# Moving tiles stored as even columns, then odd ones, and read by turns in both GEMMs of an f32 feed-forward block

## What is computed

```python
def _L0_cond_ref(x, condition, weights):
    W = weights[condition]                      # (32, 64, 64), a 64x64 matrix for each batch entry
    return jnp.einsum('bct,bcd->bdt', x, W)     # x: (32, 64, 1024)

def _L0_ffn_ref(input, inter_w, inter_b, output_w, output_b):
    h = jax.nn.gelu(jnp.einsum('bsd,df->bsf', input, inter_w) + inter_b, approximate=True)
    out = jnp.einsum('bsf,fd->bsd', h, output_w) + output_b
    return out

x = x + _L0_ffn_ref(_L0_cond_ref(x, itok_B_0_15, L0_cond_weights), ...)
```

## Time and profile before

| what | value |
|---|---|
| median of three runs | 1215.04 us |
| the profiled execution's own time | 1215.01 us |
| its span | 1213.2 us |
| TensorE busy | 1208.7 us, 100% |
| VectorE busy | 884.7 us, 73% |
| ScalarE busy | 562.6 us, 46% |
| matmul instructions in the profile | 5468 |

### The profile page before, as it was taken

The page is one execution under the profiler, slowest core; times in us unless marked ns, Lnnn a source line. Parts: engine busy times, 40 slices in busy tenths (PEclk is TensorE's granted clock), DMA queues, the critical chain, the costliest instruction groups (busy, mean ns, idle before and its releaser), DMA issues.

```text
span 1213.2 us, 15228 instructions
## 1 busy us (share of the span) xinstructions
PE 1208.7 (100%) x5468; PEld 1006.4 (83%) x5468; DVE 884.7 (73%) x1130; ACT 562.6 (46%) x963; POOL 273.4 (23%) x188
## 2 busy tenths in 40 slices
PE   9999999999999999999999999999999999999999
PEld 9888888888888888888888888888888888888887
DVE  5988787778657556665548678577788676788886
ACT  5755555555444444444445444444444444444443
POOL 4351233222306333423301121101110101101000
PEclk9999999999999999999999999999999999999999
DMA  9597667866997544665399998756863749956653
GB/s 347 170 302 250 219 238 288 289 241 219 401 394 234 143 124 125 189 184 138 91 342 306 348 271 266 208 194 157 192 178 115 188 126 243 291 186 179 191 154 107
DMA packets 119868, 267.62 MB, mean 221 GB/s; under 512 B 9938, under 2 KB 19442, under 8 KB 118386
## 3 DMA queue, kind: packets, MB, share of 16 engines
q1 hardware_dynamic: 105248, 232.81, 54.6%
q0 software_dynamic: 13824, 33.56, 16.3%
q10 hardware_dynamic: 722, 0.28, 0.1%
HBM read 174.34 MB, written 92.27 MB: 220 GB/s over the span
## 4 chain that ended last, share of the span: by engine, by line
PE 99%; DMA 0%; DVEq 0%; ACTq 0%; DVE 0%; issue 0%
PE ps L708 50%; PE ps L724 46%; PE ps L656 1%; PE ps L671 1%; PE ps L743 0%; DMA itok_sb<-in_itok_B_dram 0%; DVEq L277 0%; ACTq L918 0%; DVE out L1256 0%; DVE wdiag L1197 0%; DVEq L1197 0%
## 5 line engine op out<-in xcount | busy, mean ns | idle before, releaser
L708 PE MATMUL ps<-y,lhs 128*128 128x512 f32 x2688 | 610.9, 389 | 0.0
L708 PEld LDWEIGHTS ps<-y,lhs 128*128 128x128 f32 x2688 | 504.1, 188 | 104.4
L724 PE MATMUL ps<-rhs,lhs 128*128 128x512 f32 x2472 | 560.5, 389 | 0.0
L724 PEld LDWEIGHTS ps<-rhs,lhs 128*128 128x128 f32 x2472 | 464.0, 188 | 96.4
L901 ACT ACTIVATE lhs<-h_raw 128x512 fp32r<-128x512 f32 x208 | 131.6, 633 | 322.7 <-PE ps L724 317.5
L1091 DVE TENSOR_TENSOR lhs<-h_raw,lhs 128x512 fp32r<-128x512 f32 x208 | 144.2, 693 | 124.8 <-ACT lhs L901 124.6
L994 DVE TENSOR_TENSOR lhs<-w_raw,lhs 128x512 fp32r<-128x512 f32 x128 | 111.2, 869 | 127.7 <-ACT lhs L807 127.7
L807 ACT ACTIVATE lhs<-w_raw 128x512 fp32r<-128x512 f32 x128 | 81.0, 633 | 174.5 <-PE ps L708 172.9
L1094 DVE TENSOR_TENSOR rhs<-w_buf,rhs 128x512 fp32r<-128x512 f32 x208 | 142.4, 685 | 0.0
L906 ACT ACTIVATE rhs<-w_buf 128x512 fp32r<-128x512 f32 x208 | 128.0, 615 | 0.0
L994 DVE TENSOR_TENSOR lhs<-s_w,lhs 128x512 fp32r<-128x512 f32 x96 | 73.0, 765 | 57.4 <-ACT lhs L807 57.0
(11 more groups left out here) (54 smaller groups left out, 553.5 us busy)
## 6 DMA issues: line engine op xcount, KB each, us to landing
h_raw<-p_mem SPq DMA_DIRECT2D x80, 512.0 KB, 5.1
w_raw<-in_L_ffn_inter_w_dram SPq DMA_DIRECT2D x31, 1024.0 KB, 7.9
p_mem<-part SPq DMA_DIRECT2D x96, 256.0 KB, 6.3
w_buf<-in_L_ffn_output_w_dram SPq DMA_DIRECT2D x12, 2048.0 KB, 14.3
q_mem<-part SPq DMA_DIRECT2D x64, 256.0 KB, 6.3
h_raw<-q_mem POOLq DMA_DIRECT2D x32, 512.0 KB, 7.5
y_mem<-y_out SPq DMA_DIRECT2D x28, 512.0 KB, 3.3
y<-y_mem SPq DMA_DIRECT2D x7, 2048.0 KB, 13.5
```

The source lines that it names most:

```text
L708: last = nc.tensor.matmul(ps[:, bank, :], w[:, k, :], y[i][:, part, k, :], start=(i in FRESH and k == 0 and u == 0), stop=(k == KH - 1 and ...
L724: last = nc.tensor.matmul(ps[:, bank2(t, tb), :], lhs[s % RING][:, a, blk(tb)], rhs[r][:, w, :], start=(t in FRESH2 and q == 0 and u == 0) ...
```

## The change

Within each row of 512 words of a moving tile, columns 0, 2, 4, ... now lie first, and columns 1, 3, 5, ... behind them, 256 words (1 KB) further on. `runs` is a stored row seen as its two halves, `by_runs` a row in column order seen as even columns and then odd ones, and `by_pairs` a stored row read back in column order: a word of the first half, a word of the second, and so on. The matmuls of both GEMMs read their moving operand through `by_pairs`, so columns reach TensorE and PSUM in the same order as before. The copies that fill these tiles read their source through `by_runs`, at a step of two words, and write without gaps. For the first half of y the copies out of PSUM do this, so `y_sum`, `y_high` and `y_low` are unchanged; for the second half and for `rhs` the copies and subtractions that split the tile do it. `y1_sum` has three more waits in each of four blocks, on VectorE's own earlier subtractions. The order of the instructions is the same on every engine.

```diff
+        def by_runs(columns):
+            return columns.rearrange("p (b a) -> p a b", a=2)
+        def runs(kept):
+            return kept.rearrange("p (a b) -> p a b", a=2)
+        def by_pairs(kept):
+            return kept.rearrange("p (a b) -> p b a", a=2)
...
-                        last = nc.tensor.matmul(ps[:, bank, :], w[:, k, :], y[i][:, part, k, :],
+                        last = nc.tensor.matmul(ps[:, bank, :], w[:, k, :], by_pairs(y[i][:, part, k, :]),
...
-                        last = nc.tensor.matmul(ps[:, bank2(t, tb), :], lhs[s % RING][:, a, blk(tb)], rhs[r][:, w, :],
+                        last = nc.tensor.matmul(ps[:, bank2(t, tb), :], lhs[s % RING][:, a, blk(tb)], by_pairs(rhs[r][:, w, :]),
...
-                                                        rhs[(r + i) % RING][:, w, cols],
+                                                        by_pairs(rhs[(r + i) % RING][:, w, :])[:, cols.start // 2:cols.stop // 2, :],
...
-                    nc.scalar.activation(to[:, kb % KH, :], ps[:, kb, :], ACT.Copy).then_inc(kept_act, 1)
+                    nc.scalar.activation(runs(to[:, kb % KH, :]), by_runs(ps[:, kb, :]), ACT.Copy).then_inc(kept_act, 1)
...
-                nc.scalar.activation(rhs[r][:, 0, :], w2_part(t, q), ACT.Copy).then_inc(rhs_hi, 1)
+                nc.scalar.activation(runs(rhs[r][:, 0, :]), by_runs(w2_part(t, q)), ACT.Copy).then_inc(rhs_hi, 1)
...
-                nc.scalar.activation(y1_out[item % 2][:, 0, :], y1_in[:, (0, 0, 0, 3, 1, 2, 2)[i], :], ACT.Copy).then_inc(y1_hi, 1)
+                nc.scalar.activation(runs(y1_out[item % 2][:, 0, :]), by_runs(y1_in[:, (0, 0, 0, 3, 1, 2, 2)[i], :]), ACT.Copy).then_inc(y1_hi, 1)
...
-                    nc.vector.tensor_copy(to[:, kb % KH, :], ps[:, kb, :]).then_inc(kept_dve, 1)
+                    nc.vector.tensor_copy(runs(to[:, kb % KH, :]), by_runs(ps[:, kb, :])).then_inc(kept_dve, 1)
...
-                nc.vector.tensor_tensor(rhs[r][:, 1, :], w2_part(t, q), rhs[r][:, 0, :].bitcast(F32),
+                nc.vector.tensor_tensor(runs(rhs[r][:, 1, :]), by_runs(w2_part(t, q)), runs(rhs[r][:, 0, :]).bitcast(F32),
                                         ALU.subtract).then_inc(rhs_lo, 1)
...
+                if n in (0, 1, 3):
+                    dve.wait_ge(y1_split, kb * PRODUCTS + (1, 2, 0, 6)[n])
                 nc.vector.tensor_tensor(y1_in[:, to, :], y1_in[:, a, :], y1_in[:, b, :], ALU.subtract).then_inc(y1_t, 1)
...
-                nc.vector.tensor_tensor(o[:, 1, :], y1_in[:, (0, 0, 0, 3, 1, 2, 2)[i], :], o[:, 0, :].bitcast(F32),
+                nc.vector.tensor_tensor(runs(o[:, 1, :]), by_runs(y1_in[:, (0, 0, 0, 3, 1, 2, 2)[i], :]), runs(o[:, 0, :]).bitcast(F32),
                                         ALU.subtract).then_inc(y1_split, 1)
```

## The result

The changed kernel takes 1165.11 us (median of 4 runs, 1164.06 to 1165.9) against 1214.97 us before: a ratio of 0.9589 (95% interval 0.9572 to 0.9605), or 49.9 us less. The forecast was 2321 us.

The account below looks back on a forecast made before the run. The prediction took TensorE's matmul cadence as the bound: 1215.0 us plus 1105.9 us for the alternating moving read, with zero for copies, waits and writes, gave 2321 us. The range was 1213 to 2425 us, at 80%.

Parts of the forecast that it names:

- The bound: Whole kernel: TensorE busy 1208.7 of 1213.2 us, so time is the number of matmuls times their cadence, plus short ends.
- The split of 226.67 ns: A 512-column matmul in order: 0.4167 ns a word, 213.33 ns, plus 13.3 ns paid once per matmul at either width.
- the price of the moving read: Both GEMMs' matmuls reading alternate halves: 0.833 ns a word instead of 0.4167, adding 1105.9 us; lower bound nothing.
- F: Rival, 7%: faster; the other word order avoids a weight-load collision costing 13.3 ns per matmul, 69 us less, 1146 us.
- B: Rival, 24%: the moving read's stride is free, if the port keeps a line of each half or fetches fast enough; 1215 us.
- D: Rival, 10%: the moving port is late only now and then, giving something between, 1230 to 2146 us.
- E: Rival, 13%: moving read worse than half pace, each line change exposing the whole access; for example 2867 or 4530 us.
- The strided copies: Copies filling moving tiles at a step of two words: zero taken; upper bound 533 ns more on VectorE, 454 on ScalarE.
- part 2: The forecast's step on copies filling moving tiles: zero on the path, with groups staying at 615 and 685 ns.
- C: Rival, 2%: matmul reads free but strided copies slow, about 5 us in GEMM2 and 2 us at the head; 1222 us.
- The copies out of PSUM at the head: At the start, 16 strided copies with thin cover: zero taken; at the upper bound TensorE would wait some 1.9 us.
- The waits on VectorE's own subtractions: Three more per block of y, 12 in all: zero taken; whole subtractions exposed would be 8 us over 200 us.

## Why the prediction was wrong

**The bound.** That TensorE's cadence is the time held nearly: 5178 matmuls times the change of cadence, 55.5 us, is the busy time lost. With the faster cadence 4.8 us of new waits came up beside it.

**The split of 226.67 ns.** 0.4167 ns a word and 13.3 ns a matmul was right: alone, 384, 320 and 256 columns in order take the same 13.1 to 13.4 ns above their words (448 columns take 16.1 ns). It was drawn from one piece of 30 matmuls, so that it held was partly luck.

**The step that failed is the price of the moving read.** I bounded it below by nothing and took 0.833 ns a word from the f32 passes on line 671, on the reason that a contiguous stream can take several neighbouring words with one access and the alternating one "takes that away on every word". By the count of the table, halves by turns lose nothing of that: each of the two lines in use serves four pairs in succession, where in order a line serves two. The price was -10.7 ns a matmul, and my lower bound was on the wrong side of it. The half pace itself is real. It is 431 to 461 ns in the patterns in which a line serves one pair, against my 440 ns; I gave the right price to the wrong pattern.

**The rule of the Trainium skill.** SBUF - State Buffer, in the Trainium skill (the note on cachelines), asks for at least two hits on a 16-byte line and charges for each change of line. The turned read changes line with every word and is the fastest of all; a step of two words has its two hits on every line and runs at half pace, 452.7 ns. In both cases the measurement decides against that reading of the rule. Counting pairs fits better, with the exceptions in the table.

**The rivals.** F, at 7%, had the right sign and the wrong size and cause. It gave back all 13.3 ns, 69 us; measured are 10.7 ns, 55.5 us. The 2.5 ns that stay equal the fixed cost per matmul that the Trainium skill gives in TensorE: Matmul & The Clock Gate, under "Wait - 56ns, not 53.3ns?", and the trace agrees with 215.8 - 213.3 = 2.5 ns. F's cause, the load of the weights, is not shown. Less to load does not cut the loss at 512 columns (231.7 ns at 32 columns), while how weights and moving row are placed and stepped shifts it by up to 18 ns. bf16 in order has no such loss (215.9 ns). What exactly the stream in order waits for at each matmul stays open. B, at 24%, had the nearer time, 1215 us, and still missed by 50 us; its condition, a line of each half kept at hand, would fit the turned read but was not seen. D and E fall.

**The strided copies.** I took zero on the path. The prediction named its own test: lines 906 and 1094 should stay at 615 and 685 ns, and if not, part 2 is wrong. They went to 855 and 836 ns, so part 2 was wrong in their duration. (Its upper bound adds 533 and 454 ns to 0.97 us; the sum is 0.99 us.) With TensorE in order the copies do cost nothing on the path (1215.11 us). Beside the turned read the changed kernel is 3.5 us longer than the read alone (1165.11 against 1161.59 us), and 3.1 us in the spans of the profiled executions (1163.0 against 1159.9 us). Where it comes from is shown only in part. The cover in GEMM2 mostly held: TensorE's waits of 1.5 us there came in two places, each behind a DMA: near 640 us ScalarE had waited 4.85 us for a piece of h, near 710 us VectorE 3.6 us for an output block. The other execution of this kernel with a trace has 0.2 us. In GEMM1 the waits are 3.1 and 2.3 us in these two executions, against 1.7 us with the read alone. In the medians the lower clock of some executions may add to it. C named these copies, at 7 us; the order of size was right, the path by which it should come was not shown. C was said to decide only if the stride is free, and it showed beside a gain instead. The copies out of PSUM at the head cost nothing, as taken.

**The waits on VectorE's own subtractions.** The strided groups and the waits came together, and no run has the waits alone in the turned kernel. In the kernel with the copies alone they are present and the time is 1215.11 us, so they cost nothing there.

## What to carry to other kernels

Before a stream is called ideal, divide its piece of the chain by its count and compare with the words at full pace: of the 13.3 ns over, 10.7 ns were there to be had, 4.6% of this kernel. Where the moving operand is fp32r and TensorE is the bound, read it by turns from two halves (not from four or more), and mend the order where it is cheap, at PSUM reads and at loads of weights, rather than in copies within SBUF. Before a piece is divided by its count, see whether records are missing or a gap ends it. Do not carry the turned read to bf16, and give "nothing" as a lower bound of a cost only when a gain has been ruled out by a run.

## What the runs showed of the hardware

- fp32r, 512 columns: 215.8 ns by turns of two, 226.7 to 235.6 ns in order depending on where the operands start, 431 to 462 ns where each line serves one pair of words, 283.1 ns by turns of four and 488.1 ns by turns of eight.
- bf16, 512 columns: 215.9 ns in order, 484 ns by turns of single values, 271 ns by turns of two.
- Two accesses that cost little each can cost more together. ScalarE's strided SBUF read takes 656 ns beside a TensorE that reads in order, and 855 ns beside one that reads by turns, while an unstrided one stays at 617 ns.
- A read of PSUM at a step of two f32 words costs nothing on VectorE (1218 ns for 1024 words, beside a turned read by TensorE) or ScalarE (603 ns for 512). A write to SBUF by turns takes ScalarE 1132 ns for 512 words in place of 615 ns.
- Weights loaded at a step of two words cost the turned stream nothing (215.8 ns); at a step of four the cadence is 236.7 ns, at eight 240.5 ns.
- After a wait of 2.46 us TensorE's granted clock was 0.50 for the next 3 us (1.2 GHz), in the kernel whose copies write by turns.
